# The stage ahead of the neighbour loop of a graph attention kernel, rebuilt: where the block firsts and rows come from, who counts them, 64 degree classes, two additions per tile

## The chip, the cores and the metric

The kernel runs on one core of a Trainium2 chip as one launch. The metric is device time in microseconds, taken as the median of several runs; lower is better. A profiled execution of the same program gives the trace from which rows are read.

## The reference, cut to what matters

The layer has 6250 nodes of 256 features and 206250 edges, sorted by their destination. With x normalised per row (xn):

```
q, k, v = xn @ Wq.T + bq, xn @ Wk.T + bk, xn @ Wv.T + bv     # 8 heads of 32
sim   = (q[dst] * k[src]).sum(-1) / sqrt(32)                 # per edge and head
attn  = softmax of sim over the edges of one dst
agg   = segment_sum(attn * v[src], dst);  x += agg @ Wo.T + bo + mix(xn)
x    += ffn(layernorm(x))      # 8 experts, one per token, capacity 977
```

Here mix is a linear attention over all nodes. The mixture part, ffn, comes at the end.

## The kernel before

Nodes are held in 49 tiles of 128 (NT = 49, the last with 106 real rows). The program has three parts: a stage ahead of the loop, an edge loop over sorted nodes, and the expert part. Only the first is rebuilt; the loop gets some DMA issues.

*The tile work of the first stage.* x is loaded in seven groups of seven tiles into three buffers (load_x; groups 0 and 1 on ScalarE's queue, the others on SP's). Of each group VectorE takes statistics (L294, L297), ScalarE takes an inverse root with Ln and Exp (L301, L302), VectorE makes -mean * root (L748), and ScalarE centres each tile (L729); group 0 is centred on VectorE ahead of everything (L311). Per tile t, TensorE transposes it (L754), ScalarE copies it from PSUM (L756) and rounds it to a high half (L759), and VectorE makes the low half (L761). One tile later TensorE multiplies both halves with the halves of the joined weights (L141: 12 matmuls, 512 and 256 columns), VectorE adds the biases of key, value and query (L779, L780, L781) into one of three stage buffers, and SP writes the buffer to kv_d (rows of 520) and q_d (rows of 320, the last 64 of which are for the ids). An addition waits until the writes of the buffer three tiles back have landed. At the end of a group SP loads x for the group after next but one, and writes xn_d.

*The sort beside it.* The loop needs nodes ordered by falling degree, and each node's first edge. dst is cut into 1612 blocks of 128 edges. The kernel copies dst to dst_d in DRAM with a padded end, reads the first entry of each block (firsts), and counts how many blocks start below each node (L333 to L364, with one-hot matmuls). That names one block per node (50 columns of 128 nodes); GpSimd gathers these rows of 128 entries (take_rows, L394), and VectorE counts the entries below the node (compare L429, reduction L433), which gives first edge and degree (L436 on). Then GpSimd gathers each node's own source ids from src_d (take_own, L402); SP writes them into q_d beside the queries, amid the tiles. The degree, cut at 127, makes a class; one-hot matrices (L452) and matmuls give each class's size and each node's rank in it (13 rounds of four columns: TensorE L487, L488, VectorE L495), and one-hot matrices over the rank (L509, L519, L522) with matmuls (L531) put node, first edge and degree in sorted order. tables (L564 on) makes the loop's control tables and a mask (L684 to L691).

*The order of the work* is written out by hand. Each engine runs its instructions in program order and waits on semaphores. ranks is a Python generator: pump takes one step of it at fixed places of the tile loop, one per tile, and two from tile 22 on (WAIT_ROWS = 21). GpSimd's gathers are handed out three per tile behind a tile's product (fetch_some). From tile 16 to 31 SP also writes 16 blank pieces of 516 KB into hb_d, the experts' token buffer (one per tile).

*Into the loop.* When the last kv and q writes have landed, GpSimd gathers the first 13 columns of sorted queries with their ids (L582); SP then reads the index tables (L970), VectorE ends tables and prepares the mix weights (L809), and GpSimd starts the loop's gathers, eight of kv rows per chunk (L1041) and one of queries. The loop holds six chunks in a ring. Its turns (six chunks) are in order: turns with the sums of mix, two to join, eight "aux" turns in which mix is applied to tiles that SP loads (tile_in), and the rest.

Of the kernel before, what the change touches and what calls it, by code (L numbers as in the profile page):

```python
# [5 lines left out]
NT = 49  # L6
NP = NT * 128
E = 206250
NB = 1612
# [24 lines left out]
WAIT_ROWS = 21  # L34
PER_TILE = 3
PUMP = 2
# [34 lines left out]
def gps_layer_kernel(nc, x, src, dst, wall, ball, wmix, wqm, wout, wo, bo, b_out, gate_w, gate_b, w1, b1, w2, b2, out):  # L71
# [12 lines left out]
    with ctx:  # L84
# [31 lines left out]
        dst_d = dram("dst_d", [NBP, 128], i32)  # L116
# [4 lines left out]
        hb_d = dram("hb_d", [H * CP, HR])  # L121

# [78 lines left out]
        S.preload_act_table_set("natural_log_exp_and_others")  # L201
        t_c = g(G.memset(ident, 0.0))
# [52 lines left out]
        s_pad, s_ed, s_fi = sem("s_pad"), sem("s_ed"), sem("s_fi")  # L255
        zero = R3[:, 2048:2176]
        blank = R3[:, 3136:3136 + 4 * HR]
        bigi = R3[:, 128:256].bitcast(i32)
        t_z = v(V.memset(zero, 0.0))
        t_b = v(V.memset(bigi, 1 << 20))  # L260
# [3 lines left out]
        npad = EP - E  # L264
        dma(Y, flat(dst_d)[0:E].rearrange("(a b) -> a b", b=825), dst.rearrange("(a b) -> a b", b=825), s_ed)
        wait(Y, t_b)

        dma(Y, flat(dst_d)[E:E + 86].rearrange("(a b) -> a b", a=1), bigi[0:1, 0:86], s_ed)
        t_ed = dma(Y, dst_d[NB:NBP, :], bigi[0:NBP - NB, :], s_ed)
        assert E + 86 == NB * 128  # L270
        firsts = temp(13)
        fi_i = temp(13).bitcast(i32)
        wait(Y, t_ed)
        t_fi = dma(Y, fi_i, dst_d.rearrange("(a p) j -> p a j", p=128)[:, :, 0], s_fi, allow_slow_non_contiguous=True)
# [12 lines left out]
        t_src = dma(Y, src_d[NB:NBP, :], zero[0:NBP - NB, 0:128].bitcast(i32), s_pz)  # L287

# [19 lines left out]
        def center(xt, i, o=None):  # L308
            wait(V, (sv, sv.n))
            o = xt if o is None else o  # L310
            return v(V.tensor_scalar(out=o[:, i, :], in0=xt[:, i, :], scalar1=mv[:, 2 * i:2 * i + 1],  # L311
                                     scalar2=rs[:, i:i + 1], op0=ALU.subtract, op1=ALU.mult))

        def norm(xt, n, o=None):

            spread(xt, range(n))
            wait(V, root(n))
            for i in range(n):
                last = center(xt, i, o)
            return last  # L320

        wait(V, t_x[0])
        t_n = {(0, 6): norm(xbuf[0], 7)}


        NB13 = 13
# [39 lines left out]
        blk = temp(50)  # L366
        blki = temp(50).bitcast(i32)
        rows = R1[:, 2 * NBP:2 * NBP + 6400].bitcast(i32).rearrange("p (t j) -> p t j", j=128)
        less = r3(R1[:, 0:3200].bitcast(bf16), 128)
        fine, rp, deg = temp(50), temp(50), temp(50)  # L370
        OHf = R1[:, 0:3136].bitcast(bf16)
        OHc = r3(OHf, 128)
        of_rank = r3(R1[:, 9600:10112], 128)
# [7 lines left out]
        s_row = sem("s_row")  # L381
        QUARTERS = [(0, 13), (13, 26), (26, 39), (39, 50)]
        more = [None]
        t_kv = []

# [5 lines left out]
        def take_rows(t_blk):  # L391
            wait(G, t_blk, t_ed)
            for c in range(50):
                s_row.inc(G.indirect_dma_start(out=rows[:, c, :], out_offset=None, in_=dst_d,  # L394
                                               in_offset=bass.IndirectOffsetOnAxis(ap=blki[:, c:c + 1], axis=0)), 16)
                if c % PER_TILE == PER_TILE - 1:
                    yield

        def take_own(t_rp):
            wait(G, t_rp, t_src)  # L400
            for c in range(NT):
                t_own = s_ix.inc(G.indirect_dma_start(out=own[c // 32][:, c % 32, :], out_offset=None, in_=src_d,  # L402
                                                      in_offset=bass.IndirectOffsetOnAxis(ap=rpc[:, c:c + 1], axis=1)), 16)
                if c % PER_TILE == PER_TILE - 1:
                    yield
# [1479 lines left out]
```

## Time and profile before

| what | us |
|---|---|
| median of 3 runs | 3378.02 (3372.4 to 3378.71) |
| profiled execution, span from first to last instruction | 2949.1 |
| VectorE busy | 2429.0 (82%) |
| TensorE busy | 2127.7 (72%) |
| GpSimd busy | 2119.7 (72%) |
| ScalarE busy | 1010.5 (34%) |

The page gives the profiled execution by its span; the runs' time has some 429 us more, which lie before the first and after the last recorded instruction. Busy shares are means over stages with different limits. DMA-issuing instructions of SP are not counted as busy; GpSimd's indirect ones are. In a row of the timeline, the bracket at the end is the engine's idle time before it and what ended that.

### The profile page before, as it was taken

What the parts mean: (1) busy time and instruction counts of PE and PEld (TensorE: products, weight loads), DVE (VectorE), ACT (ScalarE), POOL (GpSimd) and SP (SyncE); (2) the same over time, 40 slices, a digit from 0 to 9 for tenths busy, and PEclk for the clock granted to TensorE, in tenths of its full rate; (3) what the DMA queues carried; (4) which work ended last, traced back from release to release, by engine and by line L of the source; (5) the groups of instructions that cost most, each with busy time, mean ns of one, the idle gap of its engine ahead of it and who ended that gap; (6) DMA issues with size and microseconds to landing.
All of it is one profiled execution on the core that took longest, in us unless ns stands there. A gap on an engine that the chain in (4) does not pass through costs nothing. (4 is left out here: it accounts for less than half of the span.)

```text
span 2949.1 us, 36213 instructions
## 1 busy us (share of the span) xinstructions
PE 2127.7 (72%) x9400; PEld 1712.6 (58%) x9401; DVE 2429.0 (82%) x3296; ACT 1010.5 (34%) x4314; POOL 2119.7 (72%) x2220
## 2 busy tenths in 40 slices
PE   5675777767776777767888876556666655599998
PEld 4473555555565666555666554444444435599997
DVE  5676788888888999999999888899999985366665
ACT  3220555556566666611111111011111114345353
POOL 4465777777777777777777777777777775567785
PEclk9796888998999999989999898887888885599999
DMA  6746777777777777788888887777777758423331
GB/s 218 246 156 172 208 210 208 207 211 217 219 218 219 218 219 218 227 233 241 257 255 257 254 241 213 212 211 211 211 211 211 211 162 288 152 70 76 88 92 15
DMA packets 257830, 587.19 MB, mean 199 GB/s; under 512 B 49410, under 2 KB 135505, under 8 KB 257565
## 3 DMA queue, kind: packets, MB, share of 16 engines
q0 software_dynamic: 150480, 467.10, 57.4%
q1 hardware_dynamic: 97947, 109.47, 11.2%
q10 hardware_dynamic: 9296, 9.44, 0.9%
q8 instruction: 37, 0.61, 0.1%
q14 instruction: 70, 0.57, 0.1%
HBM read 519.05 MB, written 71.76 MB: 200 GB/s over the span
## 5 line engine op out<-in xcount | busy, mean ns | idle before, releaser
L1041 POOL DMA_INDIRECT wide<-kv_d,arena x1099 | 1051.0, 956 | 335.0 <-issue 326.7
L1340 PE MATMUL ps<-wide,arena 128*128 128x264 f32 x2432 | 694.6, 448 | 238.9 <-DVE wide L1444 238.6
L1340 PEld LDWEIGHTS ps<-wide,arena 128*128 128x128 f32 x2432 | 530.2, 223 | 395.2 <-DVE wide L1444 283.4
L1041 POOL DMA_INDIRECT arena<-kv_d,arena x539 | 515.3, 956 | 164.3 <-issue 159.1
L1176 ACT ACTIVATE ps<-wide 128x256 f32 x229 | 88.8, 388 | 1324.2 <-DVE arena L1410 1282.5
L1413 DVE TENSOR_REDUCE arena<-arena 128x64 f32<-128x2048 f32 x229 | 523.5, 2286 | 7.9
L1340 PE MATMUL ps<-arena 128*128 128x264 f32 x1216 | 350.4, 451 | 128.7 <-DVE arena L1444 128.7
L1410 DVE TENSOR_TENSOR arena<-wide,ps 128x2048 f32<-128x2048 f32 x153 | 349.3, 2283 | 105.7 <-DMA wide<-kv_d,arena 105.6
L1340 PEld LDWEIGHTS ps<-arena 128*128 128x128 f32 x1216 | 267.0, 225 | 209.0 <-DVE arena L1444 152.9
L1444 DVE TENSOR_TENSOR wide<-wide,ps 128x2112 f32<-128x2112 f32 x152 | 356.8, 2347 | 24.4 <-ACT arena L1191 24.4
L141 PE MATMUL ps<-halves 128*128 128x256 f32 (+2 forms) x2304 | 361.9, 319 | 3.2 <-DVE halves L1703 1.6
L141 PEld LDWEIGHTS ps<-halves 128*128 128x128 f32 x2304 | 331.4, 192 | 31.1 <-POOL halves L1713 3.5
L1256 PE MATMUL ps<-arena 128*128 128x256 f32 x528 | 147.0, 427 | 89.9 <-ACT arena L1133 89.7
L1410 DVE TENSOR_TENSOR arena<-arena,ps 128x2048 f32<-128x2048 f32 x76 | 173.5, 2282 | 36.5 <-DMA arena<-kv_d,arena 36.5
L1146 ACT ACTIVATE arena<-arena 128x64 f32<-128x64 f32 x784 | 197.8, 334 | 3.2
L1138 ACT ACTIVATE arena<-arena 128x64 f32<-128x64 f32 x784 | 188.8, 242 | 3.1
L1444 DVE TENSOR_TENSOR arena<-arena,ps 128x2112 f32<-128x2112 f32 x76 | 178.4, 2347 | 0.0
L1256 PEld LDWEIGHTS ps<-arena 128*128 128x128 f32 x528 | 106.0, 211 | 114.0 <-ACT arena L1133 54.9
L1809 DVE TENSOR_TENSOR halves<-arena,halves 128x978 fp32r<-128x978 f32 x64 | 97.2, 1528 | 66.4 <-ACT halves L1807 66.4
L1138 ACT ACTIVATION_READ_ACCUMULATOR arena<-arena 128x1 f32 x784 | 146.2, 186 | 0.0
L141 PE MATMUL ps<-rear_halves,row_halves 128*128 128x512 f32 (+1 forms) x392 | 119.3, 378 | 31.6 <-DVE row_halves L761 31.4
L1848 POOL DMA_INDIRECT out<-arena x48 | 80.1, 1668 | 78.4 <-DVE arena L1845 37.8
(310 smaller groups left out, 3137.8 us busy)
## 6 DMA issues: line engine op xcount, KB each, us to landing
wide<-kv_d,arena POOLq DMA_INDIRECT x1099, 3.8
arena<-in_w SPq DMA_DIRECT2D x16, 1024.0 KB, 5.4
kv_d<-wide SPq DMA_DIRECT2D x49, 260.0 KB, 2.2
arena<-xn_d SPq DMA_DIRECT2D x82, 128.0 KB, 3.4
arena<-kv_d,arena POOLq DMA_INDIRECT x539, 3.8
hb_d<-arena SPq DMA_DIRECT2D x16, 516.0 KB
q_d<-wide SPq DMA_DIRECT2D x49, 128.0 KB, 2.7
xn_d<-arena SPq DMA_DIRECT2D x7, 896.0 KB, 9.0
```

Of the source, the lines that this page charges most:

```text
L141: m = T.matmul(o, l, r, start=(first and i == 0), stop=(last and i == len(pairs) - 1))
L1041: e.indirect_dma_start(out=kvb[k][:, j, :], out_offset=None, in_=kv_d, in_offset=bass.IndirectOffsetOnAxis(ap=ixb[k][:, j:j + 1], axis=0)) ...
L1138: m = e.activation(o[:, 64 * h:64 * h + 64], raw[:, 64 * h:64 * h + 64], ACT.Square, accum_out=ssq[:, h:h + 1])
L1146: m = e.activation(o[:, 64 * h:64 * h + 64], raw[:, 64 * h:64 * h + 64], ACT.Copy, scale=rr_[:, h:h + 1])
L1176: return e.activation(q_ps, qsf[:, bass.ds(val(e, qa, NT * QI), 256)], ACT.Copy)
L1256: m = e.matmul(o, xw_[slot][:, i, :], W0[:, i, c:c + 256], start=(i == 0), stop=(i == 1))
L1340: m = e.matmul(psE[(k + 1) % 3][:, 0:264], ident, kvb[b][:, j, 256:ROW], start=(j == 0), stop=(j == J - 1))
L1410: e.tensor_tensor(prod.rearrange("p (j n) -> p j n", n=256), kvb[k][:, :, 0:256], q_ps.unsqueeze(1).to_broadcast([128, J, 256]), ALU.mult) ...
L1413: e.tensor_reduce(S_ps[:, 0:8 * J], prod.rearrange("p (n d) -> p n d", d=32), AX.X, ALU.add).then_inc(e_red, 1)
L1444: e.tensor_tensor(kvv[b], kvv[b], p3.unsqueeze(3).to_broadcast([128, J, 8, 33]), ALU.mult).then_inc(e_pv, 1)
L1809: t_hs[e * 8 + f] = v(V.tensor_tensor(hl[:, f, 0:CE], hf[f % 2], hh[:, f, 0:CE].bitcast(f32), ALU.subtract))
L1848: t_yq[q] = s_ye[q % 4].inc(G.indirect_dma_start(out=out, out_offset=bass.IndirectOffsetOnAxis(ap=rows_[:, jj % 4, 256:257].bitcast(i32), ...
```

## The change

Firsts are read straight from dst at the very start, in three strided reads on SP, and dst_d is gone. The chain from firsts to counts stands ahead of the statistics of group 0. The row gathers are addressed by an edge offset (block * 128, at most E - 128) into dst itself and all 50 are issued at once behind that chain, by quarters with a semaphore each. ScalarE counts: Sign(entry * -1 + node - 0.5) with an accumulator gives (below - above), from which the first edge is offset + 64 + half the sum; two columns per tile from tile 7 on, three from tile 27, each quarter from the tile named in LANDED. ranks starts at tile 31, with two steps per tile; its own-row gathers are issued at once. Classes are 64. Rank rounds are seven of eight columns, with a product and a reduction on VectorE instead of one operation per column. Group 0 is centred on ScalarE like the others. The joined weights are now in the order key, query, value, so key and query leave in one addition of 512; the query's scale is folded into the halves' making. The writes of the ids into q_d and the first queries stand behind the last tile (first_queries); their wait for hb_d and for kv in tables is gone. One blank piece is written to DRAM (blank_d) at the start, and SP copies it 16 times into hb_d within the loop, two per aux turn.

```diff
-WAIT_ROWS = 21
-PER_TILE = 3
+CLS = 64
+LANDED = ((7, 13), (14, 26), (21, 39), (27, 50))
+SORTED_FROM = 31
...
+        t_f0 = v(V.memset(fi_i[:, 12:13], 1 << 20))
+        dma(Y, fi_i[:, 0:12], dst[0:whole].rearrange("(a p j) -> p a j", p=128, j=128)[:, :, 0], s_fi, ...)
+        wait(Y, t_f0)
+        dma(Y, fi_i[0:rest_, 12:13], dst[whole:whole + rest_ * 128].rearrange("(p j) -> p j", j=128)[:, 0:1], s_fi, ...)
+        t_fi = dma(Y, fi_i[rest_:rest_ + 1, 12:13], ..., s_fi)
...
-        dma(Y, flat(dst_d)[0:E].rearrange("(a b) -> a b", b=825), dst.rearrange("(a b) -> a b", b=825), s_ed)
-        wait(Y, t_ed)
-        t_fi = dma(Y, fi_i, dst_d.rearrange("(a p) j -> p a j", p=128)[:, :, 0], s_fi, ...)
+        wait(Y, t_em)
+        t_bl = dma(Y, blank_d, blank, s_bl)
-        wait(V, t_x[0])
-        t_n = {(0, 6): norm(xbuf[0], 7)}
...
+        t = v(V.tensor_scalar(out=off, in0=blk, scalar1=128.0, scalar2=float(E - 128), op0=ALU.mult, op1=ALU.min))
+        t_off = v(V.tensor_copy(blki, off))
+        wait(G, t_off)
+        for q, (c0, c1) in enumerate(QUARTERS):
+            for c in range(c0, c1):
+                s_row[q].inc(G.indirect_dma_start(out=rows[:, c, :], out_offset=None, in_=dst.rearrange("(a b) -> a b", b=825),
+                                                  in_offset=bass.IndirectOffsetOnAxis(ap=blki[:, c:c + 1], axis=1)), 16)
+        def count_some(n):
+            for _ in range(n):
+                wait(S, (s_row[q], s_row[q].n), t_half)
+                counted[1] = a(S.activation(less[:, c, :], rows[:, c, :], ACT.Sign, bias=nodeh[:, c:c + 1], scale=-1.0,
+                                            accum_out=fine[:, c:c + 1]))
...
-                t = v(V.tensor_tensor(less[:, c0:c1, :], rows[:, c0:c1, :], nodeid..., ALU.is_lt))
-                t = v(V.tensor_reduce(fine[:, c0:c1], less[:, c0:c1, :], AX.X, ALU.add))
+            t = v(V.scalar_tensor_tensor(out=rp, in0=fine, scalar=0.5, in1=half, op0=ALU.mult, op1=ALU.add))
...
-            for q in range(14):            # 13 rounds of 4 columns, 128 classes
+            for q in range(8):             # 7 rounds of 8 columns, 64 classes
+                        T.matmul(b[:, i * CLS:(i + 1) * CLS], start_[0:CLS, c:c + 1].to_broadcast([CLS, 128]), ident[0:CLS, 0:CLS], ...)
+                        m = T.matmul(b[:, i * CLS:(i + 1) * CLS], trib, OHc[:, c, :], start=False, stop=True)
-                        t = read[u] = v(V.scalar_tensor_tensor(..., accum_out=rankf[:, c:c + 1]))
+                    t = read[u] = v(V.tensor_tensor(of_rank[:, 0:n, :], ..., OHc[:, 8 * u:8 * u + n, :], ALU.mult))
+                    t = v(V.tensor_reduce(rankf[:, 8 * u:8 * u + n], of_rank[:, 0:n, :], AX.X, ALU.add))
...
+        def first_queries():
+            wait(Y, *t_own_)
+            dma(Y, ids_of[:, 0:32, 256:QI], own[0].bitcast(f32), s_own)
+            t_ids = dma(Y, ids_of[:, 32:NT, 256:QI], own[1].bitcast(f32), s_own)
+            wait(G, *t_sorted, t_ids, *t_kv)
+            for c in range(FIRST_Q):
+                (s_q0 if c < RING else s_q).inc(G.indirect_dma_start(out=qi[:, c, :], ..., in_=q_d, ...), 16)
...
-                if t > WAIT_ROWS:
-                    pump()
+                count_some(min(2 + (t >= LANDED[3][0]), landed - counted[0]))
+                if t == SORTED_FROM:
+                    more[0] = ranks()
+                pump()
-                    fetch_some(tm)
-                    v(V.tensor_tensor(stage[u % 3][:, 0:256], b0[:, 0:256], bal[:, 0:256], ALU.add))
-                    v(V.tensor_tensor(stv[u % 3][:, :, 0:32], r3(b0[:, 256:512], 32), r3(bal[:, 256:512], 32), ALU.add))
-                    t_bias[u] = v(V.tensor_tensor(stage[u % 3][:, 520:776], b1_[:, 0:256], bal[:, 512:768], ALU.add))
+                    v(V.tensor_tensor(both[u % 3], r3(b0[:, :], 256), r3(bal[:, 0:512], 256), ALU.add))
+                    t_bias[u] = v(V.tensor_tensor(stv[u % 3][:, :, 0:32], r3(b1_[:, 0:256], 32), r3(bal[:, 512:768], 32), ALU.add))
-                    if 16 <= u < 32:
-                        t_hz = dma(Y, hb_d[i * 512:(i + 1) * 512, :].rearrange("(p j) d -> p (j d)", p=128), empty, s_hz)
...
+        while len(t_sorted) < 2:
+            pump()
+        first_queries()
...
+            def blanks():
+                e.dma_start(hb_d[bass.ds(val(e, hz, H * CP - 512), 512), :].rearrange("(p j) d -> p (j d)", p=128), blank_d).then_inc(s_hz.h, 16)
+            for _ in range(2):
+                blanks()
             with aligned(e, mybir.EngineType.SP, AUX - 1):
                 e.reg_add(bs, bs, 16)
+                for _ in range(2):
+                    blanks()
                 for k in range(RING):
```

## Rows read from the trace of the kernel before

**Rows 1.** The page's first line.

```profile
span 2949.1 us, 36213 instructions
```

**Rows 2.** Stretches: start:end, length, busy us (instructions) per engine, then PEclk, DMA, GB/s.

```profile
core 0: us, PE busy (x) PEld busy (x) DVE busy (x) ACT busy (x) POOL busy (x), PEclk, DMA share, GB/s
46.00:71.00 25.00, 19.59 (x105) 16.67 (x104) 13.20 (x43) 9.34 (x23) 19.09 (x20) 0.86 0.75 243
...
1500.00:1600.00 100.00, 83.60 (x313) 61.47 (x314) 98.17 (x114) 12.63 (x59) 75.87 (x80) 0.92 0.86 256
```

**Rows 3.** Timeline of the start: start us, us, engine, line, operation.

```profile
0.87 1.28 ACT L201 ACT_TABLE_LOAD   x1 [0.71 <-PEq L1875]
...
6.86 2.38 DVE L294 BATCH_NORM_STATS2 arena<-wide 128x6 f32<-128x256 f32 x7 [2.04 <-DMA wide<-in_x]
...
11.37 0.40 SPq L136 DMA_DIRECT2D arena<-dst_d  x1
...
15.03 0.17 DVE L333 CAST arena<-arena 128x13 f32<-128x13 int32 x1 [1.46 <-DMA arena<-dst_d]
...
21.18 0.25 DVE L364 TENSOR_SCALAR arena<-wide,arena 128x50 f32<-128x50 f32 x1
...
25.82 0.79 PE L141 MATMUL ps<-rear_halves,row_halves 128*128 128x512 f32 x1 [1.33 <-DVE row_halves L761]
...
33.27 1.16 POOL L394 DMA_INDIRECT wide<-dst_d,arena  x1 [29.57 <-PE ps L754]
```

**Rows 4.** Timeline of VectorE over the tiles and the sort.

```profile
58.18 0.43 DVE L779 TENSOR_TENSOR wide<-ps,wide 128x256 f32<-128x256 f32 x1 [4.56 <-DMA q_d<-wide]
...
71.19 0.43 DVE L779 TENSOR_TENSOR wide<-ps,wide 128x256 f32<-128x256 f32 x1 [1.13 <-PE ps L141]
...
82.60 0.42 DVE L779 TENSOR_TENSOR wide<-ps,wide 128x256 f32<-128x256 f32 x1 [4.44 <-DMA q_d<-wide]
...
95.19 0.43 DVE L779 TENSOR_TENSOR wide<-ps,wide 128x256 f32<-128x256 f32 x1 [1.15 <-PE ps L141]
...
103.47 1.89 DVE L429 TENSOR_TENSOR wide<-wide,arena 128x1664 bf16<-128x1664 int32 x1 [6.76 <-DMA wide<-dst_d,arena]
...
127.20 0.21 DVE L436 SCALAR_TENSOR_TENSOR arena<-arena 128x50 f32<-128x50 f32 x1
...
162.94 0.42 DVE L779 TENSOR_TENSOR wide<-ps,wide 128x256 f32<-128x256 f32 x1 [1.29 <-PE ps L141]
...
168.66 0.42 DVE L779 TENSOR_TENSOR wide<-ps,wide 128x256 f32<-128x256 f32 x1 [1.19 <-PE ps L141]
...
244.18 0.42 DVE L779 TENSOR_TENSOR wide<-ps,wide 128x256 f32<-128x256 f32 x1 [1.00 <-PE ps L141]
```

**Rows 5.** Groups by line, 25 to 246 us: busy, mean ns, idle before.

```profile
L729 ACT ACTIVATE wide<-wide,arena 128x256 f32<-128x256 f32 x42 | 24.1, 588 | 26.4 <-DVE arena L748 26.4
...
L779 DVE TENSOR_TENSOR wide<-ps,wide 128x256 f32<-128x256 f32 x49 | 20.7, 422 | 43.9 <-PE ps L141 32.3 <-DMA q_d<-wide 11.6
```

**Rows 6.** Timeline from the last tile to the loop.

```profile
248.64 0.95 POOL L582 DMA_INDIRECT wide<-q_d,arena  x1 [26.94 <-DVE arena L592]
...
261.48 6.65 POOL L582 DMA_INDIRECT wide<-q_d,arena  x1 [0.30 <-issue]
...
262.86 3.68 DVE L685 TENSOR_TENSOR arena<-arena 128x3200 bf16<-128x3200 f32 x1
...
272.61 0.95 POOL L1041 DMA_INDIRECT wide<-kv_d,arena  x1 [0.30 <-issue]
```

**Rows 7.** DMA issues, 25 to 246 us: count, size, median us to landing.

```profile
xn_d<-arena SPq DMA_DIRECT2D x6, 896.0 KB, 9.3
...
q_d<-arena SPq DMA_DIRECT2D x1, 544.0 KB, 8.5
```

**Rows 8.** Waits, 1500 to 1900 us (total, times, longest), and one timeline row.

```profile
DVE arena L1410 <- DMA wide<-kv_d,arena: 16.8, 13, 2.9
...
300.47 0.24 ACT L1138 ACTIVATE arena<-arena 128x64 f32<-128x64 f32 x1
```

More of the change, by code:

```diff
@@ L389, in pump, with ranks @@
                     more[0] = None
[L391 to L400, printed above, removed]
+        def ranks():
+            wait(V, counted[1])
+            t = v(V.scalar_tensor_tensor(out=rp, in0=fine, scalar=0.5, in1=half, op0=ALU.mult, op1=ALU.add))
+            wait(V, t)
+            v(V.tensor_tensor(deg[:, 0:NT], rp[:, 1:50], rp[:, 0:NT], ALU.subtract))
+            t = v(V.tensor_copy(rpc[:, 0:NT], rp[:, 0:NT]))
+            wait(G, t, t_src)
             for c in range(NT):
@@ L491, in ranks @@
                     u = q - 1
+                    n = min(8, NT - 8 * u)
                     wait(V, made[u], t)
[L493 to L496 removed]
+                    t = read[u] = v(V.tensor_tensor(of_rank[:, 0:n, :], r3(ps[5 + 2 * (u % 2)][:, 0:n * CLS], CLS), OHc[:, 8 * u:8 * u + n, :], ALU.mult))
+                    wait(V, t)
+                    t = v(V.tensor_reduce(rankf[:, 8 * u:8 * u + n], of_rank[:, 0:n, :], AX.X, ALU.add))
                 yield
@@ L574, in tables @@
             t_ds = v(V.tensor_copy(permS[:, 0:NT], fx))
-            while not t_kv:
-                yield
-            assert t_own_
-            wait(V, t_hz, *t_own_, *t_kv)
-            t_q49 = v(V.memset(qi[:, NT, :], 0.0))
-            wait(G, t_q49, t_ds, *t_own_, *t_kv)
-            for c in range(FIRST_Q):
-                (s_q0 if c < RING else s_q).inc(G.indirect_dma_start(out=qi[:, c, :], out_offset=None, in_=q_d,
-                                                                     in_offset=bass.IndirectOffsetOnAxis(ap=permS[:, c:c + 1], axis=0)), 16)
+            t_sorted.append(t_ds)
+            t_sorted.append(v(V.memset(qi[:, NT, :], 0.0)))
+            wait(V, t_bl, t_src)
             yield
@@ L682, in tables @@
             yield
-            wait(V, t_hz)
             v(V.memset(maskT[:, :, :, J], 0.0))
@@ L710, in gps_layer_kernel @@
         xq = [r3(HX[:, 512 * i:512 + 512 * i], 256) for i in range(2)]
+        both = [R2[:, 9984 + 776 * i:9984 + 776 * i + 1040].rearrange("p (a b) -> p a b", b=520)[:, :, 0:256] for i in range(3)]
         t_lo, t_mm = {}, {}
@@ L733, in gps_layer_kernel, with minus_mean @@
         s_hz = sem("s_hz")
-        empty = blank
+        def minus_mean():
+            return v(V.scalar_tensor_tensor(out=nmr, in0=r3(mv, 2)[:, :, 0], scalar=-1.0, in1=rs, op0=ALU.mult, op1=ALU.mult))
+        t_n = {}
+        wait(V, t_x[0])
+        spread(xbuf[0], range(7))
+        wait(V, root(7))
+        t_nm[0] = minus_mean()
+        for i in range(2):
+            t_n[0, i] = center_s(xbuf[0], i, t_nm[0])
+        wait(V, t_w)
+        v(V.tensor_scalar(out=bal[:, 256:512], in0=bal[:, 256:512], scalar1=SC, scalar2=None, op0=ALU.mult))
+        wait(V, t_wh)
+        v(V.scalar_tensor_tensor(out=wl[:, :, 256:512], in0=W[:, :, 256:512], scalar=SC, in1=wh[:, :, 256:512].bitcast(f32),
+                                 op0=ALU.mult, op1=ALU.subtract))
+        v(V.tensor_tensor(wl[:, :, 0:256], W[:, :, 0:256], wh[:, :, 0:256].bitcast(f32), ALU.subtract))
+        t_W = v(V.tensor_tensor(wl[:, :, 512:768], W[:, :, 512:768], wh[:, :, 512:768].bitcast(f32), ALU.subtract))
+        wait(V, t_W)
         for grp in range(7):
```

171 lines of the change are left out of this document (68 added, 103 removed).

## The prediction

> **What bounds the kernel now.** I read the page's heading first: one core, a span of 2949.1 us [rows 1]. The median of the runs shown is 3378.02 us, so 428.9 us lie around the span; the page gives no other time for the profiled execution, and I carry those 428.9 us over unchanged. The view of stretches comes next. In the neighbour loop, from about 272 us to 2400, GpSimd issues 80 gathers in 100 us [rows 2], one each 1.25 us, and the reader is to see that this holds although VectorE is 98% busy in the same stretch. So the loop has GpSimd's issue as its pace, and nothing of that pace is edited: what the stage ahead of the loop gains or loses arrives one to one at the end. The timeline of that stage then gives its joints: first product at 25.82 us, row gathers from 33.27, ranking arithmetic from 127.20, first addition of the last tile at 244.18 (its rows leave at 245.3, after three additions of 0.42 us, partly overlapped [rows 5]), first gather of the loop at 272.61 [rows 3, 4, 6]. In between no engine is full; what ends last changes. Early it is the stage buffers: one addition per group of seven tiles waits 4.44 or 4.56 us for an older q_d write [rows 4]. Then the rows: VectorE stands 6.76 us for them at 103.47. Later TensorE: with two ranking steps per tile the tiles come 5.72 us apart (162.94 and 168.66) [rows 4].
>
> **The change part by part.**
>
> *Start.* Before, the block firsts wait for a copy of dst in DRAM: their read goes out at 11.37 and VectorE uses it at 15.03, 3.7 us later. Now three reads go out first of all on SP; the third follows a memset and two issues of 0.4 us (the price of the one at 11.37), so about 2.5 us, and lands at 6.2 by the same 3.7. The chain from there to the counts took 21.18 + 0.25 - 15.03 = 6.4 us: 12.6. Three small operations of 0.2 us each follow, and the 50 gathers may start at 13.2 instead of 33.27 [rows 3]. Behind that chain VectorE now has the statistics of group 0 (2.4 us, 3 with the aggregates), ScalarE the root and three centring passes of 0.59 us before the first eviction [rows 3, 5]; then come transposes, eviction, the hi and lo halves. From the end of the statistics to the first product I estimate 4.6 us (three passes and some four operations of 0.4 to 0.6), with the three small operations 8.4 us in all, so the first product comes at 21.0, 4.8 us earlier. Bounds: the firsts could land at 5 us or, beside the x and weight loads, at 9: first product at 19.8 to 23.8. The weight halves lie beside this, on VectorE while ScalarE centres.
>
> *Tiles 0 to 30.* Up to tile 20 I keep the old spacing: 95.19 - 25.82 = 69.4 us, which gives 90.4. Gathers ran in most of that stretch before, too (50 of them, 1.25 us apart), so their traffic is already in that spacing. The counting of rows goes to ScalarE, two or three operations per tile. A 128x64 activation with accumulator takes 0.24 us [rows 8]; at twice the width I take 0.30 (the fixed part doesn't double), so 0.6 to 0.9 us per tile; doubled whole it would be 0.48. ScalarE was busy 9.34 of 25 us [rows 2], and nothing waits behind a count except the next centring and eviction, which wait for TensorE's transposes: no cost. If that cover is gone the price is 50 x 0.30 = 15 us. The counts can't stand waiting for rows: quarter by quarter they are called for at tiles 7, 14, 21, 27 (about 46, 70, 94 and 114 us, counted back and on from 90.4 at 3.43 us per tile), and the last gather goes out at 13.2 + 50 x 1.25 = 76. So the stand of 6.76 us goes, and with it the compare and reduce passes on VectorE (1.89 us per 13 columns each [rows 4]). What is late next there is the old stage-buffer wait. One addition for key and query instead of two saves an instruction's fixed part, a fraction of its 0.42 us; the additions wait for TensorE or for buffers anyway, so nothing (if that cover goes, at most 49 x 0.42 = 20 us gained). From tile 20 to 30 are ten tiles at (95.19 - 71.19)/7 = 3.43 us: 34 us, so ranking starts near 124, against 127.20 before: nearly the same moment, but with 18 tiles left and not 24.
>
> *Ranking and sorting.* Before, this took 245.3 - 127.2 = 118.1 us. Six tiles fewer lie in it. A tile's own cost is at most 2.8 us (the 24.0 us of a group without the 4.44, by seven) and at least 1.7 (four VectorE operations of 0.42 [rows 5]); I take 2.3: -14. The four one-hot passes have 64 and not 128 classes; a pass of 128x1664 elements took 1.89 us in the compare of the same shape [rows 4], so four cost 6.9 and half goes: -3.4. The rank rounds go from 13 of four columns to 7 of eight. On VectorE 49 short operations become seven products and seven reductions of 512 elements, 0.58 us each at the rate of that compare; on TensorE columns are half as wide, but there are as many weight loads. Tiles 5.72 apart with eight columns each become four tiles with sixteen: gain between 0 (weight loads set the pace) and 11 (half); no row shows a 64-column product, I take 4. So 118.1 - 14 - 3.4 - 4 = 96.7: the last rows leave at 220.7, 24.6 us earlier. The 49 own-row gathers now go out in one piece, 61 us from about 125, well before that.
>
> *From the last tile to the loop.* Here the change costs. Before, the last rows left at 245.3 and the first query gather came at 248.64, 3.3 us later. Now the two writes of the own ids into q_d, which earlier lay amid the tiles, are issued on SP behind the last kv, q and xn writes, and POOL's first query waits for them. The second id write alone took 8.5 us to land and a xn write 9.3 [rows 7]. So the wait lies between 8.5 + 1.2 = 9.7 us (behind three issues of 0.4, the transfers overlapped) and 9.3 + 8.5 = 17.8 (one after the other); I take 12.5, because the xn figure includes loads that are not there at the end. Queued behind this wait on POOL are the 13 queries and then every gather of the loop. The slow query gather, 6.65 us beside VectorE's mask pass at 262.86 [rows 6], stays: the mask comes about 16 us after the last tile as before, and the queries are then still under way. So first loop gather at 220.7 + 27.3 + 9.2 = 257.2 instead of 272.61: -15.4 us. The table chain itself starts earlier, as it no longer waits for the kv writes, but it isn't last.
>
> *Blank writes of hb_d.* They go from SP amid the tiles to SP in the eight aux turns of the loop, two per turn, now from DRAM to DRAM. DMA share there is 0.86 at 256 GB/s [rows 2], POOL does not wait for them, and VectorE waited for gathers 16.8 us in 400 [rows 8]; a tile_in queued behind them has a turn to land. I take 0. The upper end, if all 16 x 0.53 MB, read and written, push gathers aside at 256 GB/s: 66 us. The lower end is that the first stage gets this traffic back; that is a rival below.
>
> Sum: 2949.1 - 15.4 = 2933.7 in the span, and with 428.9 around it 3362.6 us.
>
> **A rule weighed.** The trace has a single table load, 1.28 us, at the start [rows 3]; Sign is new on this engine. The Trainium skill (ScalarE: Activation LUTs, "Table sets: the hidden batching unit") says that tables come as named sets, that relu, copy, identity and abs are filler in all of them, and that changing sets reloads; Sign isn't in that list. No run here shows yet which holds. By the rule the time would be that of the second rival.
>
> **Rivals.**
> 1. *Sort bound by its own steps.* The ranking is 37 steps in a fixed order; if these and not the tiles set the 118 us, six tiles fewer bring nothing: 118.1 - 7.4 = 110.7, end of tiles at 234.7, plus 9.2 in the tail: -1.4, 3377 us. For it: VectorE and TensorE wait for each other throughout. Against: steps are issued two per tile, and in the rounds TensorE has the tile's own products in its 5.72 us.
> 2. *Table reloads.* If Sign and Ln/Exp exclude each other, three groups' roots fall among the counts, two loads each: 6 x 1.28 = 7.7 us in the chain of statistics, root, centring: 3370 us. Against it: ScalarE has slack, but not at that joint.
> 3. *Traffic.* Without blanks, and with the rows in by 80 us, the 4.44 us wait of each group goes for four groups: another 17.8 us, 3345. Against: x load, xn write and q write stay in one queue, and the wait stood at 58 us as well, before any blank.
> 4. *Slower: the blanks in the aux turns.* With VectorE 98% busy and DMA at 0.86 in that stretch the gathers arrive late, the ring of six empties and VectorE's lost time isn't given back. Half of the 66 us gives 3395. It decides from 15.4 + 6.8 = 22 us on, 1.4 us per blank. For it: the aux turns have the highest DMA rate of the loop. Against: the wait of only 16.8 us in 400, and six chunks of cover.
>
> **Numbers.** Forecast 0.57, rival 1 0.15, rival 2 0.08, rival 3 0.08, rival 4 0.12. A difference under 0.2%, 6.8 us, can't be told from no change here. Faster: 0.57 without 0.05 for its upper edge, half of rival 2, and rival 3: 0.64. Same 0.24, slower 0.12. The forecast's own range is 3352 to 3375: downwards 1.2 (start), 7 (rank) and 2.8 (tail), upwards 2.8, 4 and 5.3, from the bounds above; with rivals 1 and 3 it goes to 3344 and 3382.
>
> **What would show it.** First row gather near 13 us and first product near 21; no stall of VectorE for rows; one table load; Sign operations near 0.3 us; ranking from about 124; the last tile's addition near 219.6; then about 36 us to the first gather of the loop, with POOL waiting for the id write; 80 gathers per 100 us in the aux stretch as before. I am wrong if the first gather of the loop comes after 266, or if it comes near 257 and the end has not moved by as much: then the loop has taken it.

## The result, and the profile after

The changed kernel takes 3475.93 us (median of 4 runs, 3472.71 to 3485.32) against 3377.0 (3372.4 to 3378.71): 1.0303 times as long, interval 1.0286 to 1.0319. I had forecast 3363, with a range to 3382. It is slower by 99 us, and none of my rivals gave that.

The page's first line of the kernel after, and then of the kernel before, profiled once more for the first experiment:

```profile
span 3474.0 us, 36211 instructions
```

```profile
span 3364.2 us, 36213 instructions
```

The reader is to see two things. The span of after is its own time less 1.2 us (3475.16); that of before in the second profile is its time less 1.2 us, too (3365.38). So nothing like 428.9 us lies around a span, and the profile that I predicted from, with its 2949.1 us [rows 1], was of an execution that ran differently from all the timed ones. From here on after is compared with the second profile of before.

Joints of the front, all of them start times (us) read from the timelines. The columns are the kernels that the experiments below explain.

| | before, first | before, again | after | b1 | c1 | c2 | c4 | d2 |
|---|---|---|---|---|---|---|---|---|
| first addition | 30.1 | 31.6 | 24.6 | 25.3 | 25.1 | 24.6 | 25.5 | 25.4 |
| ranking starts | 127.2 | 137.5 | 163.1 | 137.4 | 136.4 | 137.4 | 126.8 | 111.1 |
| rank rounds, first product | 153.5 | 167.0 | 242.7 | 164.9 | 163.8 | 166.6 | 152.8 | 135.8 |
| rank rounds over | 193.0 | 206.5 | 299.8 | 215.9 | 191.7 | 221.3 | 207.5 | 160.4 |
| sorted order there | 239.7 | 253.9 | 348.0 | 264.1 | 238.9 | 269.6 | 255.4 | 206.4 |
| last tile's addition | 244.2 | 258.4 | 346.3 | 262.4 | 237.1 | 267.9 | 253.7 | 218.2 |
| first query | 248.6 | 262.9 | 361.0 | 277.1 | 251.9 | 272.4 | 268.8 | 222.8 |
| loop's first gather | 272.6 | 286.0 | 388.9 | 304.9 | 279.8 | 295.9 | 296.2 | 246.1 |
| loop's last gather | 2382.2 | 2776.2 | 2884.4 | 2804.2 | 2773.8 | 2800.2 | 2786.3 | 2741.8 |

Before again to after: the loop starts 102.9 us later and lasts 5.3 us longer (2495.5 against 2490.2). In b1 to d2 the loop lasts 2490 to 2504 us, so those 5.3 us tell nothing: the whole loss lies in the front. The stretches of after that hold GpSimd's two runs of gathers, and one of the loop (columns as in [rows 2]):

```profile
14.00:78.00 64.00, 17.07 (x72) 13.04 (x72) 13.40 (x50) 7.85 (x19) 48.06 (x50) 0.71 0.35 111
164.00:226.00 62.00, 16.75 (x87) 11.93 (x86) 9.19 (x22) 2.64 (x7) 47.12 (x49) 0.55 0.25 61
1500.00:1600.00 100.00, 70.08 (x266) 55.55 (x265) 82.14 (x91) 50.80 (x261) 60.13 (x64) 0.82 0.62 178
```

The same of before, profiled again:

```profile
14.00:78.00 64.00, 41.75 (x193) 33.61 (x194) 30.99 (x101) 16.56 (x40) 29.80 (x31) 0.89 0.55 176
1500.00:1600.00 100.00, 58.05 (x198) 43.81 (x198) 84.33 (x96) 10.35 (x47) 60.95 (x65) 0.77 0.66 190
```

While GpSimd issues without a break (50 gathers in 62 us, 49 in 61), TensorE does 17 us of work in 64 where it did 42, the DMA engines are a quarter to a third busy, and no engine but GpSimd is full. In the first profile of before, 50 gathers went out just as densely, from 33.27 to 95.50 us, and TensorE did 51 us of work beside them:

```profile
33.00:96.00 63.00, 51.41 (x272) 43.14 (x271) 36.37 (x120) 25.50 (x64) 47.80 (x50) 0.92 0.77 254
```

So the pace of the gathers does harm only in executions like the timed ones. In the loop both kernels now issue 64 or 65 gathers in 100 us, where [rows 2] have 80. The timeline of after, its start, what stands beside the first and second run, the counts, and the way into the loop:

```profile
0.87 1.28 ACT L201 ACT_TABLE_LOAD   x1 [0.71 <-PEq L1878]
...
6.97 0.17 DVE L315 CAST arena<-arena 128x13 f32<-128x13 int32 x1 [2.28 <-DMA arena<-in_dst]
...
14.34 1.16 POOL L380 DMA_INDIRECT wide<-in_dst,arena  x1 [10.64 <-DVE wide L682]
...
20.88 0.79 PE L141 MATMUL ps<-rear_halves,row_halves 128*128 128x512 f32 x1 [0.23 <-issue]
...
31.20 0.44 PE L747 MATMUL ps<-arena,wide 128*128 128x128 f32 x2 [1.93 <-issue]
...
34.44 0.28 PE L141 MATMUL ps<-rear_halves,row_halves 128*128 128x256 f32 x1
...
51.10 0.69 DVE L775 TENSOR_TENSOR wide<-ps,wide 128x512 f32<-128x512 f32 x1 [18.81 <-issue]
...
56.70 0.38 ACT L749 ACTIVATE arena<-ps 128x256 f32<-128x256 f32 x1 [24.61 <-remote]
...
76.38 0.95 POOL L380 DMA_INDIRECT wide<-in_dst,arena  x1 [0.30 <-issue]
...
83.30 0.69 DVE L775 TENSOR_TENSOR wide<-ps,wide 128x512 f32<-128x512 f32 x1 [25.31 <-remote]
...
90.62 0.39 ACT L391 ACTIVATE wide<-wide,arena 128x128 bf16<-128x128 int32 x1
90.91 0.19 ACT L391 ACTIVATION_READ_ACCUMULATOR wide<-wide,arena 128x1 f32 x1
...
204.31 0.69 DVE L775 TENSOR_TENSOR wide<-ps,wide 128x512 f32<-128x512 f32 x1 [29.12 <-remote]
...
234.03 0.43 DVE L754 TENSOR_TENSOR row_halves<-arena,row_halves 128x256 fp32r<-128x256 f32 x1 [28.62 <-ACT row_halves L752]
...
361.01 0.95 POOL L546 DMA_INDIRECT wide<-q_d,arena  x1 [135.26 <-DVE arena L649]
...
388.88 0.95 POOL L1041 DMA_INDIRECT wide<-kv_d,arena  x1 [5.16 <-issue]
```

The start is as forecast. Then ScalarE copies at 56.70 what TensorE had transposed by 31.64, and VectorE adds at 51.10 what TensorE had ended at 34.72, into a buffer that nobody had used: the work waited for was done, and the profile names no releaser ("issue" and "remote" stand where it shows none). The last stand of each run ends 7 to 9 us after its last gather went out (76.38, 224.80).

### The profile page after: what moved, and what is told of

Read it like the earlier page. It is cut to its first block and busy times, and to the rows that moved or that the text cites. A ratio compares the mean times of both kernels' runs of the same rounds, so it can differ in the third digit from the quotient of the medians.

```text
span 3474.0 us, 36211 instructions
## 1 busy us (share of the span) xinstructions
PE 2235.5 (64%) x9400; PEld 1783.6 (51%) x9401; DVE 2407.6 (69%) x3153; ACT 1047.0 (30%) x4423; POOL 2104.1 (61%) x2220
## 5 line engine op out<-in xcount | busy, mean ns | idle before, releaser
L1340 PEld LDWEIGHTS ps<-wide,arena 128*128 128x128 f32 x2432 | 531.6, 222 | 419.3 <-issue 269.6
L1340 PE MATMUL ps<-arena 128*128 128x264 f32 x1216 | 358.6, 450 | 148.2 <-issue 125.0
L1340 PEld LDWEIGHTS ps<-arena 128*128 128x128 f32 x1216 | 266.9, 224 | 232.6 <-issue 154.1
L1410 DVE TENSOR_TENSOR arena<-wide,ps 128x2048 f32<-128x2048 f32 x153 | 348.9, 2280 | 25.6 <-DMA wide<-kv_d,arena 25.3
L1256 PE MATMUL ps<-arena 128*128 128x256 f32 x528 | 171.5, 482 | 123.6 <-ACT arena L1133 72.2
L1146 ACT ACTIVATE arena<-arena 128x64 f32<-128x64 f32 x784 | 197.8, 334 | 15.0 <-ACT arena L1143 12.4
L1256 PEld LDWEIGHTS ps<-arena 128*128 128x128 f32 x528 | 122.0, 243 | 152.5 <-issue 85.2
L1262 PE MATMUL ps<-arena 128*128 128x128 f32 x396 | 76.3, 323 | 185.3 <-remote 144.5
L1262 PEld LDWEIGHTS ps<-arena 128*128 128x128 f32 x396 | 66.1, 222 | 206.1 <-remote 157.0
L1424 DVE TENSOR_TENSOR arena<-arena,ps 128x264 f32<-128x264 f32 x230 | 96.8, 421 | 99.5 <-remote 94.3
```

The costliest lines, as they stand in the source:

```text
L1146: m = e.activation(o[:, 64 * h:64 * h + 64], raw[:, 64 * h:64 * h + 64], ACT.Copy, scale=rr_[:, h:h + 1])
L1256: m = e.matmul(o, xw_[slot][:, i, :], W0[:, i, c:c + 256], start=(i == 0), stop=(i == 1))
L1262: m = e.matmul(ps[7][:, c:c + 128], kv_sb[half][:, 128 * i:128 * i + 128], kv_sb[half][:, 256 + 128 * i:384 + 128 * i], start=False, stop= ...
L1340: m = e.matmul(psE[(k + 1) % 3][:, 0:264], ident, kvb[b][:, j, 256:ROW], start=(j == 0), stop=(j == J - 1))
L1410: e.tensor_tensor(prod.rearrange("p (j n) -> p j n", n=256), kvb[k][:, :, 0:256], q_ps.unsqueeze(1).to_broadcast([128, J, 256]), ALU.mult) ...
L1424: e.tensor_tensor(acc, acc, psE[(k + 1) % 3][:, 0:264], ALU.add).then_inc(e_sc, 1)
```

## The experiments

Theory T: gathers that GpSimd issues without a break make the others' waits end late. Rivals: blanks in the loop; something else in the rebuilt front.

**a1_before**, the kernel before unchanged, and **a2_blanks_front**, after with the blanks where they were:

```
+ if 16 <= u < 32: wait(Y, t_em); t_hz = dma(Y, hb_d[piece u - 16], blank, s_hz)
- for _ in range(2): blanks()        # in the loop, twice
```

> The kernel before, unchanged, profiled once more beside the kernel after's conditions. Theory A (the profile of before with its span of 2949.1 us is an execution of another pace than the timed ones of 3377 us; the 428.9 us that I put around the span lie inside it): span about 3376, granted clock about 0.79 to 0.80, stalls of 3 to 30 us without a releaser in the front and in the loop as in the kernel after, first gather of the loop far later than 272.61, 64 to 70 gathers in 100 us of the loop instead of 80. Rival B (428.9 us do lie around the span of before, and the kernel after has lost some 525 us inside its own): span again about 2949, clock 0.875, first gather of the loop at 272 and 80 gathers in 100 us.

> The kernel after, with the 16 blank writes of hb_d put back amid tiles 16 to 31, from the SBUF tile as before, and the table chain waiting for them; nothing else undone. My rival 4 (the DRAM to DRAM blanks in the aux turns push the loop's gathers aside) as the cause of the 99 us: time at 3377 or below, 64 to 70 gathers per 100 us in the loop go up by some 3. If the loss lies in the front (first gather of the loop at 388.88 in the kernel after): within 10 us of 3476, and first gather of the loop still after 370.

a1: 3365.38 us, span 3364.2, first gather of the loop at 286.0: theory A of that text, except that the stands in its front are short. a2: 1.0296 (1.0265 to 1.0327), first gather at 385.1. Moving the blanks costs nothing that these intervals show, and my rival 4 falls.

**b1_metered, b2_rows_metered, b3_before_burst.** b1 hands out both runs three per tile again, b2 the rows alone; b3 is the kernel before with one constant changed.

```
b1, b2:  + t_mm[u] = tm = sp.inc(m); fetch_some(tm)     # three gathers behind the tile's product
b3:      - PER_TILE = 3
         + PER_TILE = 50
```

> The kernel after, with only the pace of GpSimd's front gathers undone: row gathers and own-row gathers go out three per tile behind the tile's product, as before, instead of 50 and 49 in one piece. Theory T (while GpSimd issues indirect gathers without a pause, the waits of VectorE, ScalarE and TensorE end some 20 us late; the two bursts of 62 us, 14 to 77 and 164 to 226, cost about 100 us): VectorE's stands of 18.8, 25.3, 29.1 and 30 us go, the first gather of the loop comes at 270 to 290 instead of 388.9, the time is 0.97 to 1.00 of before. Rival R (the stands come from something else in the rebuilt front: counts on ScalarE, the 512-wide addition, the id writes at the end): stands and time stay, ratio 1.02 to 1.03.

> The kernel after, with only the 50 row gathers paced (three per tile); the 49 own-row gathers still go out in one piece. Theory T: the stands before 80 us go, those from 164 on stay beside the second burst; about half of the loss comes back, ratio 1.01 to 1.02, first gather of the loop near 335. Rival R: ratio 1.03 as the kernel after.

> The kernel before with one constant changed: 50 instead of three gathers per tile, so that rows (behind tile 0's product) and own rows (behind the tile after their indices) each go out in one piece. Nothing else of the change. Theory T: stands of 20 to 30 us appear on VectorE and ScalarE beside both bursts in a kernel that has none of the other edits, time 60 to 110 us above before, ratio 1.02 to 1.035. Rival R: within 0.3% of before.

b1: 1.0053 (1.0032 to 1.0073); b2: 1.0211 (1.0187 to 1.0234); b3: 1.0298 (1.0273 to 1.0322). One constant gives the old kernel the whole loss of the new one. VectorE in b3:

```profile
70.10 0.42 DVE L779 TENSOR_TENSOR wide<-ps,wide 128x256 f32<-128x256 f32 x1 [18.35 <-issue]
...
103.72 0.42 DVE L779 TENSOR_TENSOR wide<-ps,wide 128x256 f32<-128x256 f32 x1 [26.01 <-remote]
...
251.52 0.43 DVE L779 TENSOR_TENSOR wide<-ps,wide 128x256 f32<-128x256 f32 x1 [54.12 <-DMA q_d<-wide]
```

Theory T holds for these executions. In b2 VectorE stands 5.9 us at most beside the rows, and still 15.7 and 41.9 us beside the own rows. By the ratios row gathers are worth about 31 us (1.0303 to 1.0211) and own rows about 53 (to 1.0053). But neither comes back as far as I expected: b2's loop starts at 362.1 and not near 335, and b1, with 0.97 to 1.00 expected, is not 15 us faster than before but 18 slower. The table shows where: its ranking starts as early as that of before, its rounds last 51.0 us against 39.5, and its first query comes 13.0 us behind the sorted order against 9.0.

**c1_full_rows, c2_ids_early**, each b1 with one thing more, **c3_all**, both with earlier counts, and **c4_pause**, after with pauses in its runs.

```
c1:  - T.matmul(b[..], start_[0:CLS, c:c + 1].to_broadcast([CLS, 128]), ident[0:CLS, 0:CLS], ...)
     + T.matmul(b[..], start_[:, c:c + 1].to_broadcast([128, 128]), ident[:, 0:CLS], ...)   # rows 64 on zero
c2:  the two id writes move from first_queries to the end of take_own; own rows four per tile
c3:  both, - SORTED_FROM = 31  + SORTED_FROM = 25, three counts per tile from tile 6;
     + while not t_kv: yield        # the control tables wait for the last tile (in d2 too)
c4:  + for _ in range(2): wait(G, g(G.memset(acc, 0.0)))     # behind each of the 99 gathers
```

> The kernel after with paced gathers (b1_metered), and one thing more: the rank rounds' stationary operand goes over all 128 partitions again (rows 64 to 127 zero), the moving side keeps its 64 columns. Theory A (the sort sets the end of the front, and a column's pair of products is dearer in the 64-row form: 0.50 us at full clock against 0.33 before, so that 49 of them lengthened the rounds from 39.5 to 51.0 us): pairs near 0.33 us, rounds 40 to 43 us, first gather of the loop 8 to 11 us earlier than 304.9, ratio to before 1.001 to 1.003 against 1.0053. Rival B (the rounds are long because eight columns stand in one step, whatever their form): pairs and rounds as in b1_metered, ratio 1.005.

> The kernel after with paced gathers (b1_metered), and one thing more: the own rows are fetched four per tile and their ids written into q_d amid the tiles, as before, so that POOL's first query no longer waits for writes issued behind the last tile. Theory A (the wait of some 13 us between the sort's result at 264.1 and the first query at 277.1 is this write): first query 1 to 3 us behind the sort's result or the last q_d write, first gather of the loop near 293, ratio 1.001 to 1.003. Rival B (the last kv and q writes hold the query as long anyway): ratio 1.005.

> Both edits together with the paced gathers, and the counts moved ahead (rows are in by 100 us): ranking begins at tile 25 instead of 31. The rest of the change stays. If pacing, the 64-row form and the id writes are the whole loss, and the sort then ends before the last tile: last addition near 250, first gather of the loop at 275 to 283, ratio 0.996 to 1.000. If something else of the change costs time (the loop, blanks), it stays above 1.001 although the first gather of the loop comes at or before 286.

> The kernel after with its two runs of gathers in one piece, but behind each of these gathers GpSimd does two small memsets of a scratch tile and waits for each, so a gather goes out about every 2.3 us instead of every 1.25. It tells what makes the other engines stand. If it is that gathers come without a pause: stands of 18 to 30 us become short, the front gets shorter although the two runs take about 110 us each, ratio below 1.02. If it is that they come in one piece, however far apart: the stands last longer with the runs, ratio 1.04 to 1.06.

c1: 0.9971 (0.9957 to 0.9986); c2: 1.0023 (1.0008 to 1.0038); c3: 0.9937 (0.9913 to 0.9962); c4: 1.0013 (0.9997 to 1.003). In c1 the gain was more than twice what I expected, and c3's loop starts at 270.8, ahead of the 275 to 283 expected. The groups of the rounds' products, in before again, b1 and c1 (line, engine, operation, shape, count, busy, mean ns):

```profile
L487 PE MATMUL ps<-arena 128*128 128x128 f32 x98 | 17.6, 300 | 3.1 <-DVE wide L495 3.1
L488 PE MATMUL ps<-wide,arena 128*128 128x128 bf16 x49 | 10.7, 218 | 0.0
```

```profile
L475 PE MATMUL ps<-arena 64*128 64x64 f32 x98 | 27.2, 368 | 0.0
L477 PE MATMUL ps<-wide,arena 128*128 128x64 bf16 x49 | 10.7, 219 | 0.0
```

```profile
L476 PE MATMUL ps<-arena 128*128 128x64 f32 x98 | 14.2, 284 | 0.0
L478 PE MATMUL ps<-wide,arena 128*128 128x64 bf16 x49 | 9.5, 194 | 0.0
```

And how one column follows the other on TensorE, in b1 and then in c1:

```profile
172.51 0.43 PE L475 MATMUL ps<-arena 64*128 64x64 f32 x2
172.88 0.20 PE L477 MATMUL ps<-wide,arena 128*128 128x64 bf16 x1
173.01 0.43 PE L475 MATMUL ps<-arena 64*128 64x64 f32 x2
```

```profile
172.41 0.41 PE L476 MATMUL ps<-arena 128*128 128x64 f32 x2
172.66 0.19 PE L478 MATMUL ps<-wide,arena 128*128 128x64 bf16 x1
172.69 0.41 PE L476 MATMUL ps<-arena 128*128 128x64 f32 x2
```

At full clock a column takes 0.50 us where the stationary operand goes from 64 rows to 128 and back, 0.28 where all have 128; the old one of 128 classes took 0.33. The two passes of the float32 product start 0.16 us apart in b1 and 0.14 in c1; from the second to the bf16 product it is 0.20 against 0.11, from there to the next column 0.13 against 0.03. So the extra time lies at the changes between the forms and hardly in the 64-row product itself. The stretches of the rounds, in b1 and in c1:

```profile
164.90:215.90 51.00, 50.59 (x218) 39.50 (x217) 17.42 (x42) 5.87 (x15) 12.44 (x14) 0.67 0.16 47
163.80:191.70 27.90, 27.11 (x219) 25.11 (x218) 17.06 (x41) 5.87 (x15) 13.00 (x14) 0.94 0.30 88
```

The rounds are 23.1 us shorter in c1. The form at full clock makes 49 x 0.22 = 10.8 of that. The other 12 us go with the granted clock, whose mean is 0.67 in b1 and 0.94 in c1, though TensorE is busy nearly throughout in both. From 178 to 184 us b1 is at the lower level (0.50), where a column takes 0.79 us, and the tiles' own products between the rounds are slower as well. The low clock goes with the form: in the rounds of the kernels with 64 rows it is 0.56 (after), 0.67 (b1), 0.59 (c2) and 0.59 (c4), in those with 128 rows 1.00 (before again), 0.94 (c1) and 1.00 (d2). Why is not shown. The Trainium skill (TensorE: Matmul & The Clock Gate, "LDWEIGHTS (loading the stationary operand)") says that a weight load costs by its columns and not by its rows. The trace agrees for the load by itself (two loads of 64x128 take 0.29 us, two of 128x128 0.30); what is dearer is the distance between products of unlike rows.

c2's edit is worth 9.0 us at the loop's start. In b1 SP issues both id writes behind everything, and the query follows 12.4 us after:

```profile
264.75 7.05 SPq L137 DMA_DIRECT2D q_d<-wide  x2
...
277.11 0.95 POOL L563 DMA_INDIRECT wide<-q_d,arena  x1 [18.98 <-DVE arena L666]
```

In c4 the gathers still go out in two runs that wait for no tile. Only a pause lies between them, which makes them 1.94 us apart, and the 98 us are back:

```profile
60.17 0.96 POOL L380 DMA_INDIRECT wide<-in_dst,arena  x1 [0.27 <-POOL arena L383]
61.13 0.71 POOL L383 MEMSET arena<- 128x264 f32 x2
62.11 0.96 POOL L380 DMA_INDIRECT wide<-in_dst,arena  x1 [0.27 <-POOL arena L383]
```

So in these executions it is not the number in one piece and not the bytes, but that GpSimd goes from one gather to the next every 1.25 us.

**d2_best_front**: one memset instead of two, full rows, ranking from tile 27, id writes behind tile 43. **d1_before_rest, f1_before_pause, g1_before_small, g2_best_small, h1_before_three, h2_before_four** ask whether the loop's longer time has the same cause; each puts something small behind every gather of the loop:

```
d1: 12 x e.reg_add(idle, idle, 1)      f1: 2 x memset 128x32, each waited for
g1: 1 memset 128x1 (g2: the same in d2_best_front)      h1: 3, h2: 4 memsets 32x1, one wait per chunk
```

> The kernel after with one memset (0.33 us) behind each front gather instead of the two of c4_pause, the full 128-partition stationary operand of c1_full_rows, counts and ranking moved ahead to tile 27, and the id writes amid the tiles (behind tile 43). If a pause of a third of a microsecond is enough against the stands, and the 64-row form and the id writes are the rest of the loss: no stand over 8 us in the front, ranking from 115 to 122, last addition 225 to 240, first gather of the loop 255 to 272, ratio 0.988 to 0.995. If the pause is too short: stands of 10 to 30 us beside the two runs of gathers, ratio 1.00 to 1.02.

> The kernel before, with a rest of 12 register additions behind every gather of the neighbour loop and nothing else. It asks whether the loop's stands (first gather at 286.0, last at 2776.2 in the kernel before, 64 to 66 gathers per 100 us where 1.25 us each would be 80) have the cause that the front's had. Theory P (gathers without a pause make the other engines' waits end late, in the loop too, and a short rest of GpSimd's sequencer is enough): gaps of 4 to 9 us between gathers get rarer, loop shorter by 1 to 8%, ratio 0.93 to 0.99. Rival Q (the rest has to be longer, or the loop's stands come from its own waits): gathers are only spaced wider, loop the same or up to 5% longer, ratio 1.00 to 1.04.

> The kernel before, with two small memsets (128x32 each, waited for) behind every gather of the neighbour loop, so that GpSimd really pauses some 0.2 to 0.3 us there; in d1_before_rest the register additions had not spaced the gathers at all (1.26 us apart as before). Theory P (the loop's stands have the front's cause): gathers 1.45 to 1.55 us apart, gaps of over 3 us nearly gone, loop 2490 us down to 2370 to 2450, ratio 0.965 to 0.99. Rival Q (the loop's stands are of its own waits, or so short a pause does not help): gaps remain, loop 2550 to 2900, ratio 1.02 to 1.12.

> The kernel before, with one memset of 128x1 behind every gather of the neighbour loop, not waited for there (one wait per chunk); in f1_before_pause the two waited memsets had spaced the gathers to 2.25 us, far more than meant. Theory P (the loop's stands have the front's cause, gathers without a pause): gathers 1.35 to 1.5 us apart, fewer gaps over 3 us, loop 2300 to 2450 us against 2490, ratio 0.95 to 0.99. Rival Q (the loop's stands are not of that cause): gaps over 3 us as many as before, loop longer by the spacing, ratio 1.01 to 1.08.

> d2_best_front with the same memset in the loop. Theory P: ratio 0.94 to 0.98. Rival Q: ratio 1.00 to 1.07; the front as in d2_best_front (first gather of the loop near 246) either way.

> The kernel before, with three memsets of 32x1 behind every gather of the neighbour loop (one had hidden in the 0.30 us that lie between two gathers anyway: 1.26 us apart as before). Theory P (the loop's stands have the front's cause): gathers 1.35 to 1.45 us apart, gaps over 3 us fewer than half of the 102 of before, loop 2350 to 2450 us against 2490, ratio 0.96 to 0.99. Rival Q (the loop's stands are of another cause): about as many gaps, loop longer by the spacing, ratio 1.02 to 1.06.

> The same with four memsets: gathers 1.45 to 1.6 us apart. Theory P: gaps over 3 us nearly gone, loop 2400 to 2550 us, ratio 0.97 to 1.02, PE, VectorE and ScalarE without stands of over 5 us. Rival Q: gaps as before, loop 2700 to 2900 us, ratio 1.06 to 1.12.

d2: 0.988 (0.9858 to 0.9903), 40 us faster than before and some 140 faster than after by the ratios. A pause of a third of a microsecond is enough:

```profile
61.27 0.33 POOL L382 MEMSET arena<- 128x264 f32 x1
61.87 0.96 POOL L380 DMA_INDIRECT wide<-in_dst,arena  x1 [0.27 <-POOL arena L382]
62.83 0.33 POOL L382 MEMSET arena<- 128x264 f32 x1
...
124.31 0.69 DVE L784 TENSOR_TENSOR wide<-ps,wide 128x512 f32<-128x512 f32 x1 [5.39 <-PE ps L141]
...
246.05 0.95 POOL L1052 DMA_INDIRECT wide<-kv_d,arena  x1 [0.30 <-issue]
```

The longest stand of VectorE ahead of its tables is 5.39 us; ScalarE has one of 11.4 us without a named releaser, up to 126.29. Ranking began even earlier than I expected, at 111.1, and the sorted order is there 12 us before the last tile; the loop starts at 246.1, ahead of the 255 to 272 expected.

The loop's six runs are less clear. d1 gives 1.0002 (0.9985 to 1.0018), g1 1.0086 (1.0054 to 1.0118), g2 0.9947 (0.9927 to 0.9966): in all three the addition or the memset fitted into the 0.30 us that lie between two gathers anyway, so they tested nothing. By the ratios g2 is 0.7% behind d2, and g1 0.9% behind before; their loops last no longer by as much (2496.5 us against 2495.8, 2496.6 against 2490.2), so where that comes from is not shown. In f1, 1.4742 (1.4722 to 1.4762), the waits spaced the gathers to 2.25 us, far more than meant. h1 gives 1.0853 (1.0823 to 1.0883), h2 1.1561 (1.153 to 1.1593). GpSimd in h1:

```profile
1499.77 0.95 POOL L1046 DMA_INDIRECT arena<-kv_d,arena  x1
1500.76 0.38 POOL L1050 MEMSET arena<- 32x1 f32 x3
1501.29 0.96 POOL L1046 DMA_INDIRECT arena<-kv_d,arena  x1
```

At 1.52 us a gather, steps of over 3 us from one gather to the next fall from 102 to 34 (35 in h2, none in the first profile of before). That is theory P's half: the stands become rarer and give back some 280 us. But the shorter steps grow from 1.28 to 1.63 us on average, which costs some 560 us over 1638 gathers, and the loop goes from 2490 to 2772. So the loop time and the ratio that theory P gave were missed. The first profile of before has gathers every 1.25 us in the loop, too, and no such step at all. Whether the loop's stands have the front's cause is likelier by this, not shown.

## Why the prediction was wrong, step by step

- **"428.9 us lie around the span."** Wrong: 1.2 us do. A span 13% shorter than the runs' median meant that the profile was of another course, and every spacing that I took from it was that course's. As both kernels carry the same 428.9 us, that term alone would not have turned the sign; the spacings are the next point.
- **Tiles 0 to 30, "their traffic is already in that spacing", and the own rows "in one piece", both at no cost: the step that failed.** I counted GpSimd's bytes and its own time, but not what gathers without a break do to the other engines' waits in a timed execution; the wait of every third gather on a product, which the change takes away, had kept that short. The cost is 84 us (b1 against after), by c4 98. In the first profile 50 gathers go out from 33.27 to 95.50 us without harm, so its rows could not show the price. In the second the same gathers take 70 us, 34.7 to 104.7, with four steps of 2.9 to 3.5 us among them: there the wait acts as a brake when TensorE is late.
- **Ranking and sorting, 96.7 us.** For the rounds I took a gain of 4 between 0 and 11; I had no row of a 64-row operand, and a loss was outside my bounds. Measured in b1: 11.5 us longer, so 125.0 us from ranking to the last addition where before takes 120.9. With full rows (c1) it is 100.7, 20.2 less than before against the 21.4 forecast, but that agreement is in part luck. The rounds give 11.6 and not 4. From their end to the sorted order it is 47.2 us against 47.4, and 46.0 to 48.3 in every column of the table, however many tiles lie in it. So fewer tiles bring nothing there: in that stretch the mechanism of rival 1 holds, and the sort is bound by its own steps.
- **From the last tile to the loop, +9.2.** The wait for the id writes was near: the last rows leave at 263.4 in b1, and the first query follows 13.7 us later for the 12.5 that I took. But from the last addition to the loop's first gather it is 42.5 in b1 against 27.6 before, +14.9: 10.2 ahead of the first query and 4.7 behind it. SP reads the index tables once the first six queries have landed; in b1 the two slow queries (5.95 and 2.62 us) are the second and third, in before the last two, so GpSimd now stands 5.1 us ahead of its first gather. With the id writes amid the tiles (c2) the stretch is 28.0, although there, too, the sorted order (269.6) comes behind the last addition (267.9).
- **Start.** First gather at 14.34 for 13.2, first product at 20.88 for 21.0. **Counts:** 0.38 us apart (90.62, 91.00) for 0.30, hidden. **Ranking starts** at "nearly the same moment": 137.4 in b1 and 137.5 before.
- **Table loads.** One, at 0.87, in the whole span. Rival 2 falls with the rule behind it as I read it: Sign makes no reload beside Ln and Exp here.
- **Blanks at 0, loop's pace unchanged.** Right (a2; 64 and 65 gathers per 100 us), though the pace was not the 80 that I took.

Together: 84 us for the runs, 28 for the 64-row form with the clock that goes with it (b1 to c1), 10 for the id writes (b1 to c2, ratios times 3374) make 122, where the whole loss is 102 by the same ratios. So the rest of the change was worth some 20 us, if the three add up. The forecast for it was 24.6, as the 15.4 of its sum had 9.2 for the id writes taken off. c3, which has none of the three but ranks six tiles earlier, shows 21.

## What to carry to other kernels

A metering wait that looks like lost time can be what keeps the other engines going: before taking it away, ask who runs in the pause, and if the wait goes, keep a pause (a memset of 0.33 us behind each gather was enough here). A profile whose span falls far short of the timed runs has to be explained before its spacings are used. Halving an operand's rows is not a saving to be taken for granted; look for a row of that very form.

## What the runs showed of the hardware

In the timed executions gathers that GpSimd issues every 1.25 us hold up waits of VectorE, ScalarE and TensorE by 18 to 30 us in the front, with DMA engines 25 to 35% busy; every 1.56 us (d2) they hold up none of VectorE's by over 5.4. The pace is not the whole cause: in the first profile of before the same pace came without such stands, in the front (33.27 to 95.50 us) and in the loop. Why is open. One thing goes with the stands. The first profile of before holds 44,305 records of semaphore updates, the second, of the same program, 15,502, and that of after 15,009. From 40 to 80 us, beside the first run of gathers, after has 63, c4 with its pauses 649. Where the loop's gathers are spaced, records are there again: 41,774 in f1, 42,158 in h1, 45,531 in h2. So the paths on which updates or their records travel may be full. Every run of the experiments has a recorded span, so none shows what the stands would be without recording. The Trainium skill (NOTIFIC — the notification-queue block, "7.1 Overflow: three behaviours, one of which stalls the engine") says that the inner stages of the recording, when full, hold up what feeds them rather than lose a record; no run here shows whether that is at work. The other thing not expected is the price of changing between 64-row and 128-row stationary operands, 0.22 us per column at full clock, and the lower clock beside it.
